# Scatters set singly, routing moved up, causal zeros by GpSimd selects, maxima masked on TensorE and taken from whole banks

## The reference

```python
scores = jnp.where(causal, -jnp.inf, einsum('bhtd,bhsd->bhts', q, k) * scale)
seq_out = softmax(scores) @ v
outer = Jw[..., :, None] * Jw[..., None, :]          # 6 x 6 per token and head
M_all = decayed cumulative sum of outer over earlier tokens
score_M = rd . M_all . rd                            # and score_M2 = |rd . M_all|^2
gated = mean over heads of sigmoid(mem_score * mem_scale) * gate
x = layernorm(x + (seq_out + gated * mem_val) @ out_w.T + out_b)
logits = x @ wr + br                                 # top 2 of 4 experts, softmax gates
out = sum over the two of gate * (expert(x) + constants)
x = layernorm(x + out)
```

## Time and profile before

| | |
|---|---|
| median of 3 runs | 1144.14 us (1140.71 to 1146.69) |
| the profiled execution | 1146.64 us, its span 1144.9 us |
| mean granted TensorE clock | 0.93 of full speed |

### The profile page before, as it was taken

The page is one execution under the profiler, slowest core; times in us unless marked ns, Lnnn a source line. Parts: engine busy times, 40 slices in busy tenths (PEclk is TensorE's granted clock), DMA queues, the critical chain, the costliest instruction groups (busy, mean ns, idle before and its releaser), DMA issues.

```text
span 1144.9 us, 28049 instructions
## 1 busy us (share of the span) xinstructions
PE 968.0 (85%) x8044; PEld 698.7 (61%) x8045; DVE 828.7 (72%) x2944; ACT 492.3 (43%) x1047; POOL 427.8 (37%) x374
## 2 busy tenths in 40 slices
PE   3689998797897897988879874999999999999940
PEld 1244656455454554555555553898989989999830
DVE  3647789497596795895965786777777777777737
ACT  4045464463462553644526552433333343333314
POOL 8206245265074262352743723122323323223231
PEclk8689999899898998998989886999999999999975
DMA  5742103303213213023015022123323323233347
GB/s 163 171 137 63 51 20 92 78 19 118 55 47 100 61 64 106 1 86 83 20 61 236 31 100 74 30 48 46 53 49 46 51 43 54 46 46 52 50 88 242
DMA packets 70121, 85.29 MB, mean 74 GB/s; under 512 B 18504, under 2 KB 61000, under 8 KB 69000
## 3 DMA queue, kind: packets, MB, share of 16 engines
q1 hardware_dynamic: 55728, 62.29, 18.8%
q0 software_dynamic: 14304, 21.90, 10.3%
HBM read 48.13 MB, written 35.91 MB: 73 GB/s over the span
## 4 chain that ended last, share of the span: by engine, by line
PE 64%; DVE 11%; issue 7%; DMA 5%; ACT 5%; SPq 4%; POOL 2%; another core or an unknown queue 1%; DVEq 0%; ACTq 0%; POOLq 0%
PE st L1239 8%; PE sm L1239 8%; PE sm L1250 8%; PE pv L1250 8%; PE ms L1020 6%; PE st L1060 5%; PE pv L1080 5%; PE sm L1101 3%; PE ms L999 3%; PE ms L1156 2%; PE st L1062 2%; PE ms L1128 2%; PE ms L1227 1%; DMA arena_a<-max_row 1%; PE ms L1130 1%
## 5 line engine op out<-in xcount | busy, mean ns | idle before, releaser
L913 ACT ACTIVATE arena_b<-st 128x512 f32<-128x512 f32 x320 | 188.7, 601 | 233.3 <-PE st L1062 192.4
L1464 DVE CUSTOM_DVE_ANT_0 junk<-sm,mask_ts 128x512 bf16<-128x512 f32 (+3 forms) x512 | 222.1, 486 | 55.5 <-PE sm L1101 51.5
L803 POOL DMA_INDIRECT sums<-arena_b x70 | 111.1, 1587 | 291.2 <-DVE arena_b L1720 253.3
L1060 PE MATMUL st<-arena_a 128*128 128x384 f16 (+3 forms) x512 | 137.8, 313 | 45.2 <-issue 31.0
L1101 PE MATMUL sm<-arena_a 128*128 128x512 f16 (+3 forms) x512 | 119.6, 309 | 35.3 <-DVE maxes L1464 21.9
L1700 DVE TENSOR_TENSOR arena_b<-arena_b 128x256 f16<-128x256 f32 x280 | 119.7, 427 | 9.6
L1060 PEld LDWEIGHTS st<-arena_a 128*128 128x128 f16 x512 | 51.3, 100 | 121.2 <-issue 70.7
L1698 DVE CAST arena_b<-arena_b 128x256 f16<-128x256 f32 x280 | 87.5, 312 | 41.5 <-ACT arena_b L974 39.3
L1239 PE MATMUL st<-arena_b,arena_a 128*128 128x256 f16 x840 | 115.5, 275 | 1.8 <-DVE arena_b L1674 1.8
L1250 PE MATMUL pv<-arena_a,arena_b 128*128 x864 | 116.7, 273 | 0.0
L974 ACT ACTIVATE arena_b<-st,arena_b 128x256 f32<-128x256 f32 x140 | 66.3, 474 | 116.8 <-PE st L1239 106.0
(11 more groups left out here) (246 smaller groups left out, 1685.4 us busy)
## 6 DMA issues: line engine op xcount, KB each, us to landing
arena_b<-slots SPq DMA_DIRECT2D x37, 260.0 KB
arena_a<-w SPq DMA_DIRECT2D x5, 1024.0 KB, 8.4
arena_b<-x_tr SPq DMA_DIRECT2D x8, 512.0 KB, 3.6
q_rows<-arena_b SPq DMA_DIRECT2D x32, 128.0 KB
k_rows<-arena_b SPq DMA_DIRECT2D x32, 128.0 KB
arena_a<-q_rows SPq DMA_DIRECT2D x32, 128.0 KB
arena_a<-k_rows SPq DMA_DIRECT2D x32, 128.0 KB
res<-x_tok POOLq DMA_DIRECT2D x8, 512.0 KB, 5.4
```

The costliest lines, as they stand in the source:

```text
L803: pool.indirect_dma_start(sums, bass.IndirectOffsetOnAxis(ap=token_now[:, 1 - par, m:m + 1], axis=0), y_out[1 - par][:, m, :], None, compu ...
L913: act.activation(probs[:, q, :], st_ps[piece % 2][:, :], ACT.Exp, scale=SCORE_SCALE).then_inc(exp_done, 1)
L1060: pe.matmul(out[:, at:at + width], ks[:, h % 2, h // 2, s * P:(s + 1) * P], qs[:, h // 2, s * P:T], start=m == 0, stop=False, skip_group_c ...
L1464: last = dve.tensor_tensor_reduce(junk[:, piece % 3, at:at + width], sm_ps[piece % 3][:, at:at + width], mask_ts[:, T - width:T], 1.0, NEG ...
```

## The change

- Scores: the mask matmuls go. GpSimd sets the exponentials above the diagonal to zero with `affine_select` on the four diagonal blocks of a class (512 columns; two selects where the class has two diagonals at different places), before `values`, which now wait for `masked` instead of the exponentials.
- Maxima: TensorE adds the mask into the bank (one matmul of 128 or of 2 × 128 columns), and VectorE takes the maxima of the bank's four blocks in one plain reduction. Four small reductions at the end of the 40 pieces join them by tile, ahead of the transposes.
- GpSimd follows the list: selects (`mask`), lines (`exterior`), outer products (`own`), value bias and row bias in quarters, and the scatters one at a time behind scores 32 to 39.
- Routing: `normalise` and `x1_rows` move up by about one group, `logits` from group 8 to 6, `gates` from 9 to 7, `rank` from 9 to 8.
- The load of residual rows moves from GpSimd's queue to SyncE's; one semaphore `scattered` for even, one for odd steps.

```diff
-        5: [("queries", 3), ("weights", 11), ("weights", 12), ("nothing", 1)],
-        6: [("first_weights", 0), ("normalise", 0), ("normalise", 1), ("normalise", 2), ("x1_rows", 0), ("x1_rows", 1), ("first_weights", 1), ("normalise", 3)],
-        7: [("x1_rows", 2), ("x1_rows", 3), ("first_weights", 2), ("weights", 13)],
-        8: [("logits", 0), ("memory", 0), ("memory", 1), ("first_weights", 3)],
-        9: [("gates", 0), ("rank", 0), ("weights", 14), ("weights", 15), ("nothing", 2), ("nothing", 3), ("memory", 2), ("memory", 3)],
+        5: [("normalise", 0), ("queries", 3), ("normalise", 1), ("normalise", 2), ("x1_rows", 0), ("normalise", 3), ("x1_rows", 1), ("weights", 11), ("weights", 12), ("nothing", 1)],
+        6: [("first_weights", 0), ("x1_rows", 2), ("x1_rows", 3), ("first_weights", 1), ("logits", 0)],
+        7: [("first_weights", 2), ("gates", 0), ("weights", 13)],
+        8: [("rank", 0), ("memory", 0), ("memory", 1), ("first_weights", 3)],
+        9: [("weights", 14), ("weights", 15), ("nothing", 2), ("nothing", 3), ("memory", 2), ("memory", 3)],
...
+    for n in range(12):
+        last = (4, 8, 10)[n % 3] + 10 * (n // 3) - 1
+        after(("scores", last), ("mask", n))
+    after(("lines_in", 3), ("exterior", 0), ("exterior", 1))
+    for n in range(2, 9):
+        after(("scores", 8 + n), ("exterior", n))
+    after(("mask", 4), ("own", 0))
+    for n in range(1, 9):
+        after(("scores", 18 + n), ("own", n))
+    for n in range(C):
+        after(("scores", 27 + n), ("value_bias", n))
+        after(("scores", 36 + n), ("row_bias", n))
+    for n in range(2 * C):
+        after(("scores", 32 + n), ("scatter", n))
...
+                def mask(n):
+                    g, cls = n // 3, n % 3
+                    pool.wait_ge(exp_done, n_of(40 * b + 10 * g + (4, 8, 10)[cls]))
...
+                        last = pool.affine_select(out=diagonal, in_=diagonal, compare_op=ALU.is_ge, fill=0.0, base=0,
+                                                  pattern=[[0, 4], [1, P]], channel_multiplier=-1)
+                    last.then_inc(masked, 1)
...
-                        last = pe.matmul(out[:, at:at + P], ident_b[:, :], mask_st[:, :], start=False, stop=True, skip_group_check=True)
...
-                    pe.wait_ge(exp_done, n_of(40 * b + 10 * g + (4, 8, 10)[cls]))
+                    pe.wait_ge(masked, n_of(12 * b + n + 1))
...
+                    if piece % 5 < 2:
+                        pe.matmul(out[:, 3 * P:4 * P], mask_st[:, :], ident_b[:, :], start=False, stop=True, skip_group_check=True).then_inc(sm_ready, 1)
+                    else:
+                        both = out[:, 2 * P:4 * P].rearrange("p (m s) -> p m s", m=2) if piece % 5 < 4 else \
+                            out[:, :].rearrange("p (m n s) -> p m n s", m=2, n=2)[:, :, 1, :]
+                        pe.matmul(both, mask_st[:, :], ident_b[:, :].unsqueeze(1).broadcast_to([P, 2, P]),
+                                  start=False, stop=True, skip_group_check=True).then_inc(sm_ready, 1)
...
-                        last = dve.tensor_tensor_reduce(junk[:, piece % 3, at:at + width], sm_ps[piece % 3][:, at:at + width], mask_ts[:, T - width:T],
-                                                        1.0, NEG, ALU.add, ALU.max, maxes[:, col:col + 1])
-                    last.then_inc(sm_read, 1)
+                    dve.tensor_reduce(maxes_of_blocks[:, piece // 5, piece % 5, :], sm_ps[piece % 3][:, :].rearrange("p (m s) -> p m s", s=P),
+                                      AX.X, ALU.max).then_inc(sm_read, 1)
+
+                def maxima_of_rows(_):
+                    dve.wait_ge(sm_read, n_of(40 * i + 40))
...
+                    dve.tensor_reduce(by_tile[:, :, :, 3], by_piece[:, 0:2, :, :], AX.X, ALU.max).then_inc(maxes_done, 1)
...
```

216 lines of the change are left out of this document (118 added, 98 removed).

## The result

| | |
|---|---|
| kernel before, beside the changed one | 1142.43 us (1140.42 to 1146.69, 4 runs) |
| changed kernel | 1168.55 us (1164.29 to 1171.34, 4 runs) |
| ratio, 95% interval | 1.022 (1.0174 to 1.0267): slower, by about 2% |
| spans of the profiled executions | 1144.9 and 1165.6 us |

What follows compares the result with a forecast made beforehand. A full step was taken as nearly TensorE's work plus a hole of some 10 us. −22 + 7 − 3 + 0.9 + 2 = −15, another −1, so 1128 us against the median, range 1104 to 1150.

Steps and rivals of the forecast that it cites:

- The tails: Ends of steps 2 to 7: a GpSimd chain of 15 us from exponential 33 sets the end; 22 us saved.
- hold-up: At a step's end: the block of scatters holds up the other engines, 6 to 11 us beyond step 1's.
- The bodies: Steps 2 to 7 ahead of their ends: 1.2 us a step lost, 7 us over six steps.
- the 1.3 us of VectorE's excess: In each body: 1.3 us of VectorE's added time that TensorE doesn't feel, taken off the loss.
- what the sum had as stands: At the choosing's new place: VectorE stands behind GpSimd's operations, 1.5 us a step added.
- Normalise ahead of the shift: ScalarE's queue in the body: normalise 0 makes ScalarE stand; bounds 0 and 3 us, 0 taken.
- TensorE even, maxima: Mask matmuls save TensorE 3.5 us a step, mask columns cost 3.5; bank reductions of 686 ns save VectorE 1.3.
- The selects: GpSimd's 16 selects a step: 0.75 us each, 12 us a step, hidden at no cost until a backlog forms.
- Step 8: End of step 8: the chain of 14 to 15 us, partly hidden by the weights' loading; 2 us lost.
- Step 9: Routing of the last step: two or three weight casts leave the path; 3 us gained, bounds 0 and 4.
- C: Choosing among GpSimd's small operations: VectorE stands 6 us a step instead of 1.5; 1155 us; chance 0.10.
- A: Steps 2 to 7: hold-up vanishes wholly, tails of 7 us rather than 9, body costs nothing; 1109 us; chance 0.21.

Runs made afterwards that it cites:

- order: The kernel before with nothing but the routing moved up: 1149.5 us, ratio 1.042.
- group B: Runs sharing one chip, with the kernel before repeated unchanged and traced: 1102.9 us; the changed kernel beside it 1164.2 us, ratio 1.057.
- scatters with order: The kernel before with GpSimd following the list, scatters singly, and the routing moved up; causal zeros and maxima as before: 1124.8 us, ratio 1.020.
- changed kernel less maxima: The changed kernel with the maxima put back as in the kernel before: 1163.1 us, ratio 1.056.
- normalise alone: The kernel before with only normalise and x1_rows moved up; logits, gates and rank stay: 1144.2 us, ratio 1.000.
- groups A, B and D: Three sets of runs, each on a shared chip, where the kernel before, unchanged, took 1102.3, 1102.9 and 1103.0 us.
- first pair: The first measurement of the kernel before beside the changed kernel: 1142.43 and 1168.55 us, ratio 1.022.
- scatters alone: The kernel before with only GpSimd following the list (single scatters, small pieces) and the residual load on SyncE: 1084.4 us, ratio 0.983.
- paced scatters: Scatters alone, each scatter also waiting for the exponential of the score before it: 1085.9 us (0.984), on other runs 1114.3 us (0.975).
- maxima alone: The kernel before with only the maxima changed to whole banks, scores keeping their mask matmuls: 1118.0 us, ratio 1.013.

## Why the prediction was wrong, point by point

**The tails**: right in mechanism and in size. From the end of exponential 33 the chain was to take 15 us; it took 15.0 on average, ended by values that wait for a select, no remote waits, and −25.4 us instead of −22. The 7.6 us behind the transposes, where 9.0 was forecast, says only that these come later. What failed is what the gain stood on. The 6 to 11 us that I took off are a hold-up that the kernel before has in some groups of runs only. Where it lacks it, its tails are 5.8 us, and the same chain is a loss of 11.8 us over six steps. That GpSimd's chain becomes the tail's bound was in the sum; that it is longer than the tail without scatters, 5.2 us in step 1 by my marks, stood in the trace. And the text had TensorE wait for ScalarE there; by the semaphores the lateness starts with TensorE's matmuls.

**The bodies**: the step that failed. Forecast +1.2 us a step, measured +6.7, or +5.2 up to exponential 33. The order's price, 5.6 us a body beside single scatters, is most of the miss, and two terms of the sum had it wrong. The first is the 1.3 us of VectorE's excess that TensorE was not to feel. The rows didn't give that discount: what keeps TensorE from feeling the choosing at its old place are, in part, the memory matmuls right behind the logits, and I moved the choosing away from them without naming them; its waits for the maxima grew by 2.1 us a step. The second is normalise, below. The choosing itself took 5.1 us in step 4 after, and 5.1 in step 4 of the kernel before in group B (323.24 to 328.3). But with small pieces on GpSimd it takes 3.2 us at the old place, so the new place costs it what the sum had as stands, about 1.5.

**Normalise ahead of the shift**: bounds 0 and 3, I took 0, as TensorE had work of its own there. It hadn't enough. TensorE waits 17.7 us for normalise and the queries over the six steps of the changed kernel, 2.9 a step, and 13.4 in scatters with order. The move alone measured 1.000, since there these waits replaced those for the maxima; with the choosing moved as well they add. The terms of the sum weren't independent.

**TensorE even, maxima**: 684 ns a bank against 686 forecast, right. But VectorE's saving, 2.9 us a step alone, is worth nothing in the body, and the mask columns cost what they take: 2.6 us a step alone, where 3.5 was forecast. In the changed kernel the selects' relief of TensorE pays for them, and taking the maxima back changed about 1 us.

**The selects**: 0.64 us each against 0.75, right, and nearly hidden in the bodies (−0.6 to 2.3 us each by the pairs of the table). Their price sits where GpSimd's chain ends a step: 38 us between scatters with order (1124.8) and the changed kernel less maxima (1163.1), 68 us with the old order.

**Step 8**: +2 forecast, +8.8 measured. 3.5 us lie behind exponential 33 (13.3 to 16.8): the chain was half hidden by weights in my sum, while ScalarE stood 7.53 us for it. The other 5.3 lie ahead of it, as in the bodies. **Step 9**: −3 forecast, +5.2 measured, where two traces of the kernel before differ by 2.8. The sum misread the list: it had rank ahead of weights 11 to 15, but in the new list rank stands behind weights 11, 12 and 13. No cast left the path, and one now stands between choosing and rank, 2.0 us. The rest stays open; the dummy matmuls aren't it.

**The rivals.** C named the sign and nearly the time (1155) by another mechanism. In the changed kernel the choosing takes 5.1 us, against 2.5 where nothing stood (normalise alone), so its stands are about 2.6 us and not 6; C is what the order does to the kernel before, whose biases are 2.3 us long. Its point of decision was a stand of VectorE alone; what came besides was TensorE's lost cover and its stands for normalise. A's sign, tails near 7 us behind the transposes, appeared, but by the later mark; its chain was to be 2 us shorter, and it wasn't.

**In one chain**, at the level of groups A, B and D: before 1103, scatters −18.5, order +40, selects +38, maxima +1: 1164. The shares hold for this sequence; in another they differ, as the selects' 68 us without the order show. In the first pair the kernel before carried the hold-up, some 39 us, and the changed one stood at 1168.6: +26. The order goes with the selects: with them the early routing buys tails of 9.6 instead of 13.2 us and pays with bodies of 68.7 instead of 64.6; without them it buys nothing. The best version measured is scatters alone, 0.983 where the kernel before runs at 1103; where it runs at 1140, that kernel with paced scatters is at 0.975.

## What to carry to other kernels

When a step of an engine is moved, look first at what the other engines do beside it at the old place, above all the one that sets the time: taking the memory matmuls from behind the logits cost 11 us by itself. When two moves are priced one by one, ask whether both lean on the same slack: normalise alone was free, and together with the choosing it was not. Before a wait is booked as a gain, take a second trace of the same kernel: a wait with no releaser in the profile may not be there in the next group of runs; look up in the kernel which semaphore it is for. And an operation put on an idle engine is free only until that engine's queue ends the step.

## What the runs showed of the hardware

- The same program took 1102 or 1142 us by the group of runs, with equal bodies (64.2 us) and tails of 5.8 or 13.2 us. In the long ones ScalarE and VectorE wait for up to 7.3 and 6.0 us while indirect DMAs of GpSimd run, for semaphores of TensorE's that rise up to 5.1 us behind the recorded ends of the matmuls in step 4; in the trace with the short tails no such semaphore is late by over 0.1 us. Why, no run shows.
- Small operations of VectorE lasted as long as GpSimd's operation under way: 0.55 to 0.71 us beside 256-column biases, 2.3 us beside 1024 columns. The Trainium skill (SBUF — State Buffer, "SBUF: two separate sides") has the pair of ports locked for a whole operation, also for an operation of one input in its two-port mode; the 1.13 us of L1465, which has one input, agrees. The same page of the Trainium skill ("Who interferes with whom") says that plain reductions never contend on this chip; the bank's reduction, 685 ns on average both in the changed kernel with its 128 selects and in maxima alone, which has none in its steps, agrees.
- Stands of TensorE cost more than their length: for the same matmuls 10.8 us more of busy time over six steps, where the mean granted clock was 0.96 instead of 1.00. In step 4 of scatters with order the granted clock is at its lower level, 1.2 GHz, for stretches from 321.4 and from 335.0 us, behind stands of 0.84 and 1.34 us and of 2.73 us.
